# Delta rule on one core: the 16x16 blocks solved on VectorE by way of DRAM, in a loop of four stages, and expert gathers without reused buffers

## The reference

```
def step(S, inp):
    qt, kt, vt, gt, bt = inp
    S = S * jnp.exp(gt)[..., None]
    vd = (vt - jnp.einsum('bhkv,bhk->bhv', S, kt)) * bt[..., None]
    S = S + kt[..., None] * vd[:, :, None, :]
    return (S, jnp.einsum('bhkv,bhk->bhv', S, qt))

q = causal_conv_silu(x @ Wq, ...); k = ...; v = ...
g = -exp(A_log) * softplus(x @ Wfa @ Wfb + dt_bias);  beta = sigmoid(x @ Wb)
q = l2norm(q) * SCALE;  k = l2norm(k);  o = scan(step, 0, (q, k, v, g, beta))
o = o * rsqrt(mean(o * o) + EPS) * o_norm_w * sigmoid(x @ Wga @ Wgb)
return o.reshape(b, t, D) @ Wo
```

## Time and profile before

| | |
|---|---|
| runs | 7178.68 us median of 3 (7172.1 to 7182.52) |
| the profiled execution | 7175.66 us, its span 7174.0 us |
| mean granted TensorE clock | 0.892 of full speed |
| busy: TensorE, VectorE | 5664.2 us (79%), 4624.3 us (64%) |
| busy: ScalarE, GpSimd | 2630.7 us (37%), 1854.8 us (26%) |
| delta rule, first projection to last output product | about 2096 to 5767 us |

### The profile page before, as it was taken

One profiled execution on the slowest core, in us unless ns is written; L12 is line 12 of the kernel. 1 busy time (PEld: TensorE's weight loads), 2 busy tenths in 40 slices (PEclk: granted clock), 3 DMA queues, 4 the chain that ended last, 5 costly groups with the idle time before them and its releaser, 6 DMA issues. The chain is left out here.

```text
span 7174.0 us, 88466 instructions
## 1 busy us (share of the span) xinstructions
PE 5664.2 (79%) x27189; PEld 3652.3 (51%) x27189; DVE 4624.3 (64%) x7243; ACT 2630.7 (37%) x4720; POOL 1854.8 (26%) x1756
## 2 busy tenths in 40 slices
PE   3666643799668888888888888888888867999946
PEld 1111122555346666666666666666666634555523
DVE  6899976322237776777676777676776544666666
ACT  2222211111024444444444444444444323666512
POOL 0555510020213332333332333333333222000100
PEclk7565665899879999999999999999999988999978
DMA  0321200434421000100001100000100012111110
GB/s 29 64 35 41 47 18 18 174 111 154 145 77 33 25 25 25 40 27 25 25 25 34 33 25 25 25 25 27 31 25 24 6 56 64 45 43 43 37 48 23
DMA packets 270517, 323.55 MB, mean 45 GB/s; under 512 B 28816, under 2 KB 181904, under 8 KB 268848
## 3 DMA queue, kind: packets, MB, share of 16 engines
q1 hardware_dynamic: 256192, 265.21, 12.8%
q0 software_dynamic: 13984, 54.01, 2.1%
HBM read 262.66 MB, written 56.49 MB: 44 GB/s over the span
## 5 line engine op out<-in xcount | busy, mean ns | idle before, releaser
L1546 POOL TENSOR_TENSOR delta_rule_suffix<-delta_rule_suffix,delta_rule_prefix 128x256 f32<-128x256 f32 x448 | 497.4, 1110 | 1779.0 <-ACT delta_rule_prefix L1602 1175.7
L461 PE MATMUL states_y_ps<-states_hc,main_ident 128*128 128x512 f32 x512 | 471.5, 1036 | 268.5 <-DVE states_hc L418 268.4
L434 DVE TENSOR_TENSOR_SCAN states_hs<-states_decay,states_inp 128x512 f32<-128x512 f32 x256 | 497.7, 1949 | 70.3 <-POOL states_inp L406 42.6
L1855 PE MATMUL delta_rule_level<-delta_rule_qk_second,delta_rule_k_first 128*128 128x128 f32 x3072 | 425.2, 282 | 142.2 <-DVE delta_rule_L_large L1667 126.8
L1855 PEld LDWEIGHTS delta_rule_level<-delta_rule_qk_second,delta_rule_k_first 128*128 128x128 f32 x3072 | 384.4, 194 | 193.0 <-DVE delta_rule_qk_second L1675 141.3
L2297 PE MATMUL attend_out_ps<-attend_probsT,attend_v_head 128*128 128x512 f32 x1024 | 481.5, 593 | 0.0
L406 POOL TENSOR_TENSOR states_inp<-states_du,states_bc 128x512 f32<-128x512 f32 x256 | 422.0, 1660 | 223.6 <-DVE states_hs L434 189.2
L1828 PE MATMUL delta_rule_proj<-delta_rule_hT,delta_rule_w_qkv 128*128 128x512 f32 x1024 | 476.1, 609 | 0.0
L1537 POOL TENSOR_TENSOR delta_rule_k_first<-delta_rule_qk,delta_rule_suffix 128x256 f32<-128x256 f32 x384 | 305.2, 795 | 629.1 <-PE delta_rule_level L1843 495.0
L2324 DVE TENSOR_REDUCE attend_top<-attend_scores 128x1 f32<-128x512 f32 x512 | 328.4, 683 | 159.7 <-PE attend_scores L2279 159.7
L461 PEld LDWEIGHTS states_y_ps<-states_hc,main_ident 128*128 128x128 f32 x512 | 119.9, 291 | 604.7 <-DVE states_hc L418 604.3
(11 more groups left out here) (459 smaller groups left out, 12582.0 us busy)
## 6 DMA issues: line engine op xcount, KB each, us to landing
states_bc<-bc_dram SPq DMA_DIRECT2D x128, 256.0 KB, 8.1
moe_w_d<-in_w_down SPq DMA_DIRECT2D x39, 512.0 KB, 4.2
delta_rule_w_qkv<-in_kda_wq SPq DMA_DIRECT2D x64, 256.0 KB
delta_rule_w_qkv<-in_kda_wk SPq DMA_DIRECT2D x64, 256.0 KB
delta_rule_w_qkv<-in_kda_wv SPq DMA_DIRECT2D x64, 256.0 KB
delta_rule_inv_beta<-beta_dram SPq DMA_DIRECT2D x64, 256.0 KB
delta_rule_w_o<-in_kda_wo SPq DMA_DIRECT2D x64, 256.0 KB, 4.6
parts_dram<-qkv_parts POOLq DMA_DIRECT2D x24, 512.0 KB, 6.1
```

Source lines behind the costliest of these rows:

```text
L434: dve.tensor_tensor_scan(hs[:, n % NBUF, :], decay[:, n % NBUF, :], inp[:, n % NBUF, :], 0.0, ALU.mult, ALU.add).then_inc(scanned, 1)
L461: last = pe.matmul(y_ps[k % 2][:], g["ident"][:], hc[:, n % NBUF, :], start=False, stop=(n == STATE - 1))
L1546: pool.tensor_tensor(first, first, whole_second, ALU.mult).then_inc(suffix_done, 1)
L1855: last = pe.matmul(level_ps[(i + 1) % 2][:, c, :], left, qk_second[:, i % 2, :, c * CHUNK // 2:(c + 1) * CHUNK // 2], start=True, stop=True)
```

## The change

**Delta rule.** The nine steps of the 16x16 blocks are gone. `front` fills `L_small` (now one buffer). When level 8 is in, SyncE stores the tile to `small_dram` and loads its diagonal blocks with four DMAs into `blocks`, one 16x16 block in each partition: 32 blocks for a unit, 64 for a pair of units. Once in two iterations VectorE inverts all 64 blocks there by doubling the block size, 1 to 8 (`solve`, slots 3, 5 and 7): for each size a product, a sum, a product, a sum. SyncE then writes the inverses with eight DMAs to the diagonal of `solved_dram`, which holds zeros elsewhere, waits for them, and loads both units' X from it whole.

The solve is in a stage `late`, between `middle` and `back`, together with the remaining nine steps and the gate's projection. So the loop has four stages and 67 iterations, and tiles that live longer have one more buffer. `middle` keeps the transposes of k and v.

**Around it.** Weights are loaded two units ahead, those of the output once per four units. GpSimd no longer starts X (L1554). **Experts.** The gathers go to one tile for all 32 (over the gate and up weights, once those products are done), and none waits for an addition.

```diff
-        steps = [(2, "LT", "L_small", None, COPY_A, 0, 0),
-                 (4, "L2", "LT", "L_small", COPY_A, 1, 0),
-                 (4, "L2T", "L_small", "LT", COPY_V, 1, 0),
-                 (7, "W", "L2T", "W", ADD, 2, 1),
...
-                 (10, "W", "L8T", "W", ADD, 4, 4),
+        steps = [(13, "WT", "W", None, COPY_A, 0, 0),
...
+        SOLVE_SLOTS = {3: (1, 2), 5: (4,), 7: (8,)}
...
+                def send_blocks(n):
+                    p = n % 2
+                    sp.wait_ge(small_ready, n + 1)
+                    sp.dma_start(square(g["small_dram"][p]), flat(L_small)).then_inc(small_stored, 16)
+                    sp.wait_ge(small_stored, 16 * (n + 1))
+                    reach(sp, blocks_solved, n // 2)
+                    for c, src in enumerate(diagonal(g["small_dram"][p])):
+                        sp.dma_start(block_rows(blocks, p, c), src).then_inc(blocks_loaded, 16)
+
+                def return_blocks(m):
+                    sp.wait_ge(blocks_solved, m + 1)
+                    for p in range(2):
+                        for c, to in enumerate(diagonal(g["solved_dram"][p])):
+                            sp.dma_start(to, block_rows(solved, p, c)).then_inc(solved_stored, 16)
+                    sp.wait_ge(solved_stored, 16 * 2 * CHUNKS * (m + 1))
+                    for p in range(2):
+                        reach(sp, to_state, CHUNKS * (2 * m + p - 1))
+                        sp.dma_start(flat(X[p]), square(g["solved_dram"][p])).then_inc(X_loaded[p], 16)
...
+                    def multiply(to, left, right, negate):
+                        n = len(left)
+                        prod = products[:, 0:n * s * s * s].rearrange("q (b a c k) -> q b a c k", b=n, a=s, c=s)
+                        shape = [2 * UNIT_BLOCKS, s, s, s]
+                        for b in range(n):
+                            dve.tensor_tensor(prod[:, b], left[b].unsqueeze(2).to_broadcast(shape),
+                                              right[b].rearrange("q k c -> q c k").unsqueeze(1).to_broadcast(shape), ALU.mult)
+                        dve.drain()
+                        for b in range(n):
+                            last = dve.tensor_reduce(to[b], prod[:, b], AX, ALU.add, negate=negate)
+                        dve.drain()
+                        return last
...
+                    if n % 2 == 0 and slot in SOLVE_SLOTS:
...
                             if i == 0:
-                                pe.wait_ge(state_ops_done, n + 1)
-                                pe.wait_ge(level_read, (NL + 1) * (n + 1))
+                                pe.wait_ge(X_loaded[p], 16 * (n // 2 + 1))
...
-                pipeline(front, middle, tail)
+                pipeline(front, middle, late, tail)
...
-                    if t >= 2:
-                        pool.wait_ge(gathered_added, t - 1)
```

More of the change, by code:

```diff
@@ L780, in expert_layer @@
         y_stored = [sc.sem(f"y_stored{j}") for j in range(2)]
-        gathered = [sc.sem(f"gathered{j}") for j in range(2)]
-        gathered_added = sc.sem("gathered_added")
+        gathered = [sc.sem(f"gathered{t}") for t in range(NT)]
         h_rows = g["h_dram"].rearrange("(t p) d -> t p d", p=P)
@@ L1427, in operand @@
         def operand(name, p):
[L1428 removed]
+            return {"L_large": L_large[p], "W": X[p]}.get(name) or inv[name]
         def flat(ap):
@@ new lines, in _ @@
+                load_batch(0)
+                load_unit(0)
+                load_unit(1)
+                sp.wait_ge(masks_made, 1)
+                for p in range(2):
+                    sp.dma_start(square(g["solved_dram"][p]), flat(L_small)).then_inc(background_made, 16)
+                sp.wait_ge(background_made, 32)
+                load_out(0)
+                for i in range(N + 4):
+                    if i + 2 < N:
+                        load_unit(i + 2)
+                    if i % HEADS == 4 and i // HEADS + 1 < B:
+                        load_batch(i // HEADS + 1)
+                    if i % GROUP == GROUP - 1 and 1 <= (i - 7) // GROUP < N // GROUP:
+                        load_out((i - 7) // GROUP)
+                    if i % 2 == 0 and 1 <= i // 2 <= N // 2:
+                        return_blocks(i // 2 - 1)
+                    if i < N:
+                        send_blocks(i)
@@ L1645, in back @@
                         act.activation(o_inv[:], o_inv[:], ACT.Exp, scale=-0.5).then_inc(o_inv_done, 1)
-                pipeline(front, middle, back)
+                pipeline(front, middle, late, back)
             @block.vector
@@ L1755, in middle, with solve, part @@
                 def middle(slot, n):
-                    p = n % 2
+                    pass
+                def solve(s):
+                    def part(tile, row, col):
+                        pairs = SMALL // (2 * s)
+                        return [tile[:, 2 * s * b + row * s:2 * s * b + (row + 1) * s, 2 * s * b + col * s:2 * s * b + (col + 1) * s]
+                                for b in range(pairs)]
+                    def multiply(to, left, right, negate):
[10 more added lines that the diff above has]
+                        return last
+                    middle_part = [inner[:, b * s * s:(b + 1) * s * s].rearrange("q (a c) -> q a c", a=s) for b in range(SMALL // (2 * s))]
+                    multiply(middle_part, part(blocks, 0, 1), part(solved, 1, 1), False)
+                    return multiply(part(solved, 0, 1), part(solved, 0, 0), middle_part, True)
@@ new lines, in late @@
+                def late(slot, n):
+                    p = n % 2
+                    if n % 2 == 0 and slot in SOLVE_SLOTS:
+                        for s in SOLVE_SLOTS[slot]:
+                            if s == 1:
+                                dve.wait_ge(blocks_loaded, 16 * CHUNKS * (n + 2))
+                                reach(dve, solved_stored, 16 * CHUNKS * n)
+                                for b in range(SMALL // 2):
+                                    dve.tensor_scalar(solved[:, 2 * b, 2 * b + 1:2 * b + 2], blocks[:, 2 * b, 2 * b + 1:2 * b + 2],
+                                                      -1.0, None, ALU.mult)
+                                dve.drain()
+                            else:
+                                last = solve(s)
+                            if 2 * s == SMALL:
+                                dve.engine_nop().then_inc(blocks_solved, 1)
@@ L1872, in middle, with late @@
                         last.then_inc(v_turned, 1)
+                def late(slot, n):
+                    b, h, p = where(n)
+                    if slot == GATE_SLOT:
+                        pe.wait_ge(bank_read[1], second_bank_uses(n + 2, "gate"))
+                        pe.wait_ge(wg_loaded[n % 4], 16 * (n // 4 + 1))
+                        pe.matmul(flat(proj_ps[1]), w_g[:, n % 4, :], fgT[:, b % 2, 1, :], start=True, stop=True).then_inc(gate_done, 1)
                     for i, (at, name, left, right, by, copied, added) in enumerate(steps):
```

226 lines of the change are left out of this document (127 added, 99 removed).

## The result

The changed kernel takes 7269.1 us (median of 4 runs, 7266.3 to 7273.6), the kernel before beside it 7176.4 (4 runs): 1.0129 times as long, 95% interval 1.0112 to 1.0147, or 93 us more. The forecast was 7252. All times in this document are of fast runs; one run of one experiment, 17248 us at a granted clock of 0.352, is left out.

What follows compares the result with a forecast made beforehand. TensorE was busiest at 87%, but the changed stretch was taken as paced by ScalarE's and VectorE's chain. Pairs of iterations +59, ends +19, VectorE's own copy +6 and gathers -11 made +73: 7252 us, range 7075 to 7430.

Steps and rivals of the forecast that it cites:

- VectorE's wait for its own copy: Delta rule, once a unit: VectorE waits 0.1 us for its own copy, +6 us in all.
- 3.9 us sooner at full clock: Between chunks of `back`: without the small inverse on TensorE the level product starts 3.9 us sooner, before solve and clock costs.
- The clock: Norm of k to transpose of X: sparse TensorE work halves the clock each iteration, costing 1.0 + 2.2 us.
- The solve: VectorE, slots 3, 5, 7: slot 3 hidden, 1.0 and 3.1 us show, 0.8 overlaps, in iterations with a solve.
- Iterations: Steady part of the delta rule: two lengths in turn, about 55.6 and 58.9 us; a pair loses 1.9 us.
- The way through DRAM: Blocks to DRAM and X back: time enough towards the blocks, tight on the way back, costed at nothing.
- no slack: Way back through DRAM: X arrives about 3622.8, TensorE reaches its transpose about 3623.3.
- Ends: First and last iterations: +27 us at the end with a 67th iteration, -8 in the second, together +19.
- Gathers: Expert layer: 57 us of gathers become 46, so -11 us (0 to -17).
- A: Rival: the clock holds at the 2.4 GHz level, giving 7143 us, down to 7053; chance 0.30.
- B: Rival: the way back through DRAM decides, X lands late, +198 us, so 7450; chance 0.18.
- C: Rival: clock falls with a solve and in a third of other iterations, effects cancel, 7187 us (7165 to 7193); chance 0.10.

Runs made afterwards that it cites:

- no arithmetic, extra products: Changed kernel without VectorE's arithmetic on the 16x16 blocks and with 16 added 128x128 identity products per iteration in slots 6 to 10: 6935.9 us, 0.9672.
- no arithmetic: Changed kernel without VectorE's negations and solve on the 16x16 blocks, its waits, DMAs and stages kept: 7066.5 us, 0.9856.
- With the clock held: Changed kernel with 16 added 128x128 identity products on TensorE per iteration, in slots 6 to 10: 7103.2 us, 0.9908.
- the run: Kernel before with only the expert layer's change, 32 gathers to one tile and none waiting for an addition: 7162.3 us, 0.9989.
- both remedies: Changed kernel with the solve moved to slots 0 and 3 and 16 added 128x128 identity products per iteration in slots 6 to 10: 6979.5 us, 0.9732.

## Why the prediction was right, and where it was not

The sign, the mechanism and the time were right (+93 for +73). That the time came so near is partly luck: the solve was put 99 us too low, the clock 54 too high and the gain at full clock 24 too low, and these misses nearly cancel. Between the second head and the last, in the profiled executions, each measured term being what is added to the row above:

| term | forecast | measured |
|---|---|---|
| small inverse off TensorE, full clock | -3.9 x 62 = -242 | -266 (3222.9 instead of 3489.4, no arithmetic, extra products) |
| clock | +3.2 x 62 = +198 | +144 (3366.6, no arithmetic) |
| solve | +3.3 x 31 = +102 | +201 (3567.2, the changed kernel) |
| VectorE's wait for its own copy | +6 | not measured by itself |
| sum | +65 | +78 |

Of the steps:

- **3.9 us sooner at full clock**: right. With the clock held, from ScalarE's head to the level product 24.8 us pass (3642.50 to 3667.30), and 28.7 before (3588.09 to 3616.81).
- **The clock**: right as a mechanism, 1.0 + 2.2 us in 62 iterations = 198, measured 159 or more with the solve and 132 without. Its parts were mixed up: the stretch before the level product lost more (27.2 from head to level product, so 2.4, part of it at the head), that from there to the transpose less (4.66 against 3.51 with the clock held, 1.15). The prediction said that no full iteration before had gaps that could show whether a few microseconds suffice. Each had one: ahead of the last level product TensorE waited 2.03 us, and behind that wait the clock fell to 0.50 in 32 of 57 (rows above).
- **The solve**: the term that was mis-sized. 1.0 + 3.1 - 0.8 = 3.3 us a pair, measured 6.3, and 5.5 with the extra products in both kernels (0.9908 - 0.9672). In the rows, from the norm product to the first level product 15.97 us pass with a solve (3667.00 to 3682.97) and 11.67 without (3611.64 to 3623.31), 4.3 more. Size 8 took 3.76 rather than 3.1, since its products took 1.00 and 1.07 for 0.69; size 4 delayed the scale of k by 1.3 rather than 1.0; and 0.8 came back, as forecast (without a solve the convolution of v waits 0.59 for ScalarE). Slot 3 was hidden as forecast. The other 2 us of the 6.3 lie behind the level product, where no arithmetic stands and the sum had nothing. Chunk 2's new state stood behind the convolution of v, TensorE waited 3.3 us for it, and the clock was low for 14 us instead of 7. So from the level product to the transpose 5.5 us pass in the iteration with a solve and 4.65 in the other, where without the arithmetic both have 4.1 (medians).
- **Iterations**: forecast 55.6 and 58.9, measured 56.1 and 60.0; a pair +1.9 (+2.1 with the self wait), measured +2.5. The solve was put too low and the clock too high, and the one makes up for most of the other.
- **The way through DRAM**: costs nothing, as forecast, but "no slack" was wrong. The eight stores came through 1.2 us after the last issue, not 3.7, and TensorE arrived later.
- **Ends**: +27 measured 28.4; -8 measured -10.8; 6.5 for the last reload of the output weights were missing. Gathers: -11, measured -9 in the rows and -8 in the run.
- **Rivals**: A didn't happen. With the clock held in the iterations without a solve the kernel takes 7103, inside A's 7053 to 7143, and there its 3.9 us were right; but X is in time, and the solve costs more than A had. B is excluded, C too: the clock falls in every iteration.

The Trainium skill ("TensorE: Matmul & The Clock Gate", section HAM oscillation) says that waits of a few microseconds in each round send the array back to the slow clock each time; here they did, 62 times, with waits of 2.9 and 3.3 us between single products.

## What to carry to other kernels

Work taken off TensorE out of a place where it only filled waits is worth what the chain behind it gains, less what the lost clock costs on all that follows: read the windows' clock before and after, and try a few harmless wide products in the waits before rejecting such a change. Put new VectorE work into slots where VectorE already waits and no other engine's next operand stands behind it; the same 8 us of arithmetic cost 6.3 a pair in one place and 3.3 (1.0000 - 0.9856) in another. The change with both remedies takes 6980 us, 2.7% less than the kernel before; without them it loses 1.3%.

## What was not expected of the hardware

- VectorE's product of 64x512 float32 takes 1.01 us when one operand is read with a step of 16 elements (64 bytes), 0.68 when both are read in runs of adjacent elements, a repeated operand included. With a step of 8 elements it took 1.07 in the solve. The Trainium skill ("SBUF — State Buffer", Door 1: The DMA port swizzle) says that each access to a new line of 16 bytes pays a penalty; the trace agrees for the step of 64 bytes, and shows its size.
- Sixteen products of 2 columns in an iteration, eight of them in 1.84 us, left the clock at 0.50; as many of 128 columns kept it at 1.00 in the iterations without a solve.
- A wait of 4.9 us ahead of TensorE, once a pair, made the pair 8 us longer, with the clock low again behind it.
